# Routing tiles of a gated cross-attention and expert block: the order of q, root, Exp and route transposes

## What is computed

```python
x = x + tanh(g_xattn) * xattn(layernorm(x), ctx)
x = x + tanh(g_ffn) * ffn(layernorm(x))

def xattn(q, ctx):                       # 16 heads of 16, per token
    k, v = split(ctx @ W_kv.T + b_kv)
    attn = softmax(einsum('bshd,bstd->bsht', q, k) / 4)   # heads against heads of the same token
    return einsum('bsht,bstd->bshd', attn, v) @ W_out.T + b_out

def ffn(x):                              # expert choice: 8 experts, each takes 64 of 256 tokens
    probs = softmax(x @ gate_w.T)
    g, m = top_k(probs.T, 64)            # per batch and expert
    h = gelu(x[m] @ w1[e]) @ w2[e]
    return zeros.at[m].add(g * h)
```

## Time and profile before

| what | value |
|---|---|
| median of 3 runs | 736.58 us (736.11 to 738.33) |
| profiled execution | 736.63 us, its span 734.6 us |
| granted TensorE clock, mean | 0.928 of full |
| busy: TensorE matmul | 641.7 us (87%) |
| busy: VectorE | 619.9 us (84%) |
| busy: GpSimd | 550.1 us (75%) |
| busy: ScalarE | 434.1 us (59%) |

### The profile page before, as it was taken

The page is one execution under the profiler, slowest core; times in us unless marked ns, Lnnn a source line. Parts: engine busy times, 40 slices in busy tenths (PEclk is TensorE's granted clock), DMA queues, the critical chain, the costliest instruction groups (busy, mean ns, idle before and its releaser), DMA issues.

```text
span 734.6 us, 10843 instructions
## 1 busy us (share of the span) xinstructions
PE 641.7 (87%) x3592; PEld 514.2 (70%) x3592; DVE 619.9 (84%) x726; ACT 434.1 (59%) x1077; POOL 550.1 (75%) x497
## 2 busy tenths in 40 slices
PE   5668786654799999997999999979999999999994
PEld 2334333322678888775888888758888889999994
DVE  4999999999999999889999999899999461577762
ACT  5477767643577777855777777657776533233320
POOL 3888888888868888698888887888888625445534
PEclk9988898655699999998999999989999999999997
DMA  6967774322367778766887777577777868999972
GB/s 177 345 231 259 263 242 188 125 99 75 123 182 247 237 230 231 224 201 175 243 237 230 230 237 231 185 218 206 235 229 219 268 174 271 317 308 314 308 217 29
DMA packets 97068, 160.90 MB, mean 219 GB/s; under 512 B 8171, under 2 KB 74486, under 8 KB 97014
## 3 DMA queue, kind: packets, MB, share of 16 engines
q1 hardware_dynamic: 84150, 142.91, 58.9%
q0 software_dynamic: 12288, 16.79, 12.1%
q10 hardware_dynamic: 576, 0.52, 0.2%
HBM read 126.63 MB, written 33.55 MB: 218 GB/s over the span
## 4 chain that ended last, share of the span: by engine, by line
PE 55%; DVE 21%; DMA 9%; issue 7%; POOL 6%; ACT 2%; POOLq 0%; ACTq 0%; DVEq 0%
PE bank L1017 20%; PE bank L998 20%; DVE prod_v L459 9%; DMA out_dram<-ys,ids 7%; DVE co L461 5%; PE bank L925 5%; DVE S L461 4%; PE bank L945 3%; POOL prod_p L313 2%; PE bank L986 2%; PE bank L908 2%; DMA xg<-xn_scratch,ids 1%; POOL tree_a L319 1%; POOL out_dram L379 1%; PE bank L957 1%
## 5 line engine op out<-in xcount | busy, mean ns | idle before, releaser
L998 PE MATMUL bank<-xin,w1in 128*128 128x256 f32 x1536 | 206.4, 292 | 7.6 <-issue 4.7
L998 PEld LDWEIGHTS bank<-xin,w1in 128*128 128x128 f32 x1536 | 195.8, 198 | 9.1 <-issue 8.7
L1017 PE MATMUL bank<-w2s,hT 128*128 128x256 f32 x768 | 175.4, 382 | 0.0
L379 POOL DMA_INDIRECT out_dram<-ys,ids x64 | 110.0, 1719 | 76.2 <-ACT ys L748 57.8
L1017 PEld LDWEIGHTS bank<-w2s,hT 128*128 128x128 f32 x768 | 142.4, 190 | 17.8
L738 ACT ACTIVATE hT<-bank 128x512 f32<-128x512 f32 x128 | 76.5, 598 | 117.9 <-PE bank L998 117.5
L461 DVE TENSOR_REDUCE co<-prod_v 128x208 f32<-128x3328 f32 (+2 forms) x32 | 109.7, 3428 | 1.1
L459 DVE TENSOR_TENSOR prod_v<-bank,Ex 128x3328 f32<-128x3328 f32 (+2 forms) x32 | 109.5, 3423 | 0.1
L313 POOL TENSOR_TENSOR prod_p<-kvs,q 128x1024 f32<-128x1024 f32 (+2 forms) x32 | 94.6, 2955 | 14.5 <-ACT q L706 14.5
L459 DVE TENSOR_TENSOR prod_v<-bank,q 128x3072 f32<-128x3072 f32 (+2 forms) x32 | 98.1, 3066 | 6.6 <-ACT q L706 6.6
L461 DVE TENSOR_REDUCE S<-prod_v 128x192 f32<-128x3072 f32 (+2 forms) x32 | 98.2, 3070 | 1.1
(11 more groups left out here) (123 smaller groups left out, 1079.9 us busy)
## 6 DMA issues: line engine op xcount, KB each, us to landing
w1in<-w_parts SPq DMA_DIRECT2D x128, 512.0 KB, 5.6
w2s<-in_L_ffn_w_dram SPq DMA_DIRECT2D x32, 1024.0 KB, 6.1
w_parts<-w1s SPq DMA_DIRECT2D x32, 512.0 KB, 3.5
w1raw<-in_L_ffn_w_dram SPq DMA_DIRECT2D x32, 256.0 KB, 4.4
ct<-in_ctx_dram SPq DMA_DIRECT2D x32, 128.0 KB, 4.5
xt<-in_x_dram SPq DMA_DIRECT2D x32, 128.0 KB, 4.6
out_dram<-x SPq DMA_DIRECT2D x32, 128.0 KB, 4.3
xn_scratch<-xn SPq DMA_DIRECT2D x32, 128.0 KB, 2.8
```

The lines of the kernel that those rows point to most:

```text
L379: pool.indirect_dma_start(out=out_rows[:, :], out_offset=bass.IndirectOffsetOnAxis(ap=ids[:, g % 2, p * E + e:p * E + e + 1], axis=0), in_ ...
L998: ins = pe.matmul(HB[k % 2][:, D * f:D * (f + 1)], w1in[:, k, w, c, P * f:P * (f + 1)].bitcast(f32r), xin[:, n % 2, x_, c, :], start=(m == ...
L1017: ins = pe.matmul(dst, hT[:, n % 2, f, cols], w2s[:, n % 2, f, :], start=(f == 0), stop=(f == FC - 1))
```

## The change

In routing tiles and in the step before one:

- GpSimd: `rsqrt(s + 1)` moves from before the product of `scores(s)` to between its product and its tree.
- ScalarE, step before a routing tile (s = 17, 25): `make_q(s + 1)` moves from behind `take_logits` to ahead of `take_xnT`; `gate_exp` moves ahead of `x2_stats`, with an `exp_warm` added ahead of it. At s = 9 `gate_exp` moves ahead of `take_ctT` and `x2_stats`.
- ScalarE, routing tile: `make_q(s + 1)` and `exp_warm` move ahead of `take_xnT`, `exponentials(s)` ahead of the Gelus 2 and 3, `x2_stats` ahead of `take_y`.
- TensorE, routing tile: `route_columns` moves from behind `logits` to between `hidden(n, 2)` and `hidden(n, 3)`.

```diff
--- before.py
+++ after.py
@@ -305,12 +305,14 @@
 
         @block.gpsimd
         def _(pool):
-            def share(heads, in0, in1, dst, n_tree, done):
+            def share(heads, in0, in1, dst, n_tree, done, root=None):
 
                 full = [P, heads, DK, DK]
                 in0, in1 = in0.unsqueeze(1).broadcast_to(full), in1.unsqueeze(2).broadcast_to(full)
                 pv = prod_p[:, 0:heads * DK * DK].rearrange("p (h a b) -> p h a b", a=DK, b=DK)
                 pool.tensor_tensor(pv, in0, in1, ALU.mult).then_inc(prodp_s, 1)
+                if root is not None:
+                    rsqrt(root)
                 pool.wait_ge(prodp_s, n_tree + 1)
                 src = prod_p[:, 0:heads * DK * DK].rearrange("p (r b) -> p r b", b=DK)
                 for k, buf in enumerate((tree_a, tree_b, tree_c)):
@@ -341,7 +343,7 @@
                 pool.wait_ge(kvs_ready, t + 1)
                 if t > 0:
                     pool.wait_ge(Sc_ready, t)
-                share(H - hk, Kv, qi, S[:, hk * DK:H * DK], 2 * t, Sp_done)
+                share(H - hk, Kv, qi, S[:, hk * DK:H * DK], 2 * t, Sp_done, t + 1 if routing(t) else None)
 
             def values(t):
                 hc = heads(t)[1]
@@ -416,8 +418,6 @@
             rsqrt(0)
             pool.wait_ge(bias_moved, 3 * 16)
             for s in range(NT):
-                if routing(s):
-                    rsqrt(s + 1)
                 scores(s)
                 if not routing(s):
                     rsqrt(s + 1)
@@ -808,11 +808,11 @@
                     take_low(s, 3)
                 if s >= 2:
                     take_logits(s - 2)
+                if routing(s + 1):
+                    gate_exp(s // TG - 1)
                 take_ctT(s + 2)
                 if s >= 1:
                     x2_stats(s - 1)
-                if routing(s + 1):
-                    gate_exp(s // TG - 1)
             for s in range(N0 - 1, NT):
                 n = s - N0
                 if routing(s):
@@ -824,17 +824,17 @@
                     take_kv(s + 1)
                     make_xn(s - 2)
                     x_stats(s + 2)
+                    make_q(s + 1)
+                    act.activation(exp_warm[:, :], tanh_g[:, 0:1], ACT.Exp)
                     take_xnT(s - 2)
+                    exponentials(s)
                     if n >= 0:
                         gelu(n, 2)
                         gelu(n, 3)
                     take_logits(s - 2)
-                    make_q(s + 1)
-                    act.activation(exp_warm[:, :], tanh_g[:, 0:1], ACT.Exp)
-                    exponentials(s)
+                    x2_stats(s - 1)
                     if n >= 1:
                         take_y(n - 1)
-                    x2_stats(s - 1)
                     take_xh(n + 1)
                     continue
                 if s + 1 < NT:
@@ -850,15 +850,18 @@
                 make_xn(s - 2)
                 if s + 2 < NT:
                     x_stats(s + 2)
+                if routing(s + 1):
+                    make_q(s + 1)
                 take_xnT(s - 2)
                 gelu(n, 2)
                 gelu(n, 3)
                 take_logits(s - 2)
-                if s + 1 < NT:
+                if routing(s + 1):
+                    act.activation(exp_warm[:, :], tanh_g[:, 0:1], ACT.Exp)
+                    gate_exp(s // TG - 1)
+                elif s + 1 < NT:
                     make_q(s + 1)
                 x2_stats(s - 1)
-                if routing(s + 1):
-                    gate_exp(s // TG - 1)
                 if n >= 1:
                     take_y(n - 1)
             n = n1 - 1
@@ -1088,10 +1091,11 @@
                 xn_transposes(s - 2)
                 if n >= 0:
                     hidden(n, 2)
+                if routing(s):
+                    route_columns(s // TG - 1)
+                if n >= 0:
                     hidden(n, 3)
                 logits(s - 2)
-                if routing(s):
-                    route_columns(s // TG - 1)
                 if n >= 1:
                     outputs(n - 1, 1)
                 if routing(s):
```

## The result

| | changed kernel | kernel before | ratio, 95% interval |
|---|---|---|---|
| first measurement | 729.99 us (727.61 to 730.63, 4 runs) | 737.46 us | 0.9888 (0.9849 to 0.9926) |
| second, `after_again` below | 726.75 us (726.27 to 727.19, 4 runs) | 736.74 us | 0.9864 (0.9846 to 0.9882) |

The change is 7.5 us faster in one measurement and 10.0 in the other, against 7.1 forecast. The profiled execution of the first took 727.61 us (span 725.6), 9.0 less than the one of the kernel before; it was the fastest of its four. Its timelines run 0.9 us later from the first tiles on (`con` of tile 17 ends at 309.4 and not at 308.5), so 0.9 must be taken off its times where they are set beside those of before.

The account below looks back on a forecast made before the run. TensorE bounds ordinary stretches; around routing tiles 18 and 26 VectorE's chain does, with GpSimd's ending close ahead. Removing two waits, 2 x (2.20 + 1.36) = 7.1 us, from 736.6 gave 729.5; range 725.5 to 733.0.

Parts of the forecast that it names:

- The two waits: Tiles 18 and 26: VectorE's waits for ScalarE's Exps ahead of `gsum` (2.20 us) and `den` (1.36) go, 7.1 us in all.
- One bound: Tile 18: tokens copied about 331.9, low part due 331.94; if GpSimd's chain ended last, the gain is 3.03, not 3.56.
- Both chains must shorten: Routing tiles: GpSimd's gather chain ends only some 2 us ahead of VectorE's, so a gain needs both shorter.
- a remark: Tile 18: the gather, issued earlier, no longer starts under the two additions or beside the w2 load; 3.56 us taken.
- The rival by which a change of table costs as much again: ScalarE: the gate's Exp gains 1.0 us instead of 2.2 in two tiles, giving 732.0; chance 0.04.
- TensorE's clock: Rival: behind the gaps of tiles 18 and 26 the clock stays at 2.4 GHz, 2.3 and 1.4 us more, 725.8; chance 0.17.
- a fall one stage early: Rival: the route transposes' wait, if over about 1.5 us, halves TensorE's clock from hidden 3 on, giving 740.7; chance 0.05.
- Tile 10: Tile 10: GpSimd already waits for `ids` and VectorE has no wait to lose; 0 gained, bounds -0.3 and +0.3 us.

Follow-up runs that it names:

- after_again: The changed kernel once more, unedited: 726.75 us, 10.0 us under the kernel before.
- undo_gate_exp: Changed kernel with the gate's Exp back behind the statistics, without the tiny Exp: 730.63 us, 3.9 us slower than the changed kernel.
- undo_exp_ahead: Changed kernel with the scores' Exp and the tiny Exp back behind Gelus 2 and 3 and the logits' copy: 736.25 us.
- only_q_root: Kernel before with only q ahead of the transposed copy and the root between product and tree: 735.47 us, -1.4 to before.
- only_gate_exp: Kernel before with only the gate's Exp and the tiny Exp ahead of the statistics: 740.70 us, +3.8 to before.
- undo_root: Changed kernel with the root back ahead of the 12-head product: 744.31 us, +7.6 to the kernel before.
- undo_root_w2_late: Changed kernel with the root back ahead of the product and, in routing tiles, the w2 load held until the gather has landed: 737.08 us.
- before_fill: Kernel before with 24 and 10 extra matmuls, results unread, around the token transposes of tiles 18 and 26: 733.23 us, -3.7 to before.
- undo_route: Changed kernel with TensorE's route transposes back behind logits: 730.85 us, 3.9 us slower than the changed kernel.
- heads2_gather_first: Changed kernel; in routing tiles VectorE takes 2 heads' scores, GpSimd 14, and the output additions come behind the weighted values: 735.25 us.
- heads3: Changed kernel; in routing tiles VectorE takes 3 heads' scores and GpSimd 13: 729.34 us, 2.1 us slower than the changed kernel.

## Why the prediction was right, and where it was not

**The two waits.** Right, as forecast. With 0.9 us taken off for the later start, the changed kernel's trace has the 12-head product at 304.1 (304.2 forecast), the gather at 324.5 (324.55), `hidden` at 332.6 (332.7), and 0.76 us of wait at the route transposes (0.6). `undo_gate_exp` and `undo_exp_ahead` bring back waits of 1.38 and 2.87 us. One bound was less close than forecast: I had the tokens copied just when VectorE's low part is due, with the 4.93 us of the earlier trace rows. The transfer took 3.96, and the copy ended about 1 us ahead of the low part (331.70 and 332.75).

**Both chains must shorten.** Right, and stronger than I had it. GpSimd's part alone gains 1.4 us (`only_q_root`), the gate's Exp alone loses 3.8 (`only_gate_exp`), and all of the change but the root's new place loses 7.6 (`undo_root`). The size of a late gather was wrong in what I expected of `undo_root`: I priced it by its delay, and the trace showed that it also meets the w2 load and takes 7.1 us. What I had given as a remark, that the gather no longer runs beside that load, is worth 4 us a tile once the gather is that late (`undo_root_w2_late`).

**The tables.** The rival by which a change of table costs as much again is out. In the changed kernel's rows above, the load of 1.28 at 324.87 begins 0.02 us after the Exp ends, and the Gelu starts at 326.17, 0.02 us after the load; the trace does not bear out the drain of about 1.38 us given by the Trainium skill (ScalarE: Activation LUTs, "What ACT_TABLE_LOAD costs"). The measured row decides.

**TensorE's clock.** This is the step that failed. I gave 0.17 to the case that the clock stays at 2.4 GHz in both tiles, took it as falling in the sum, and argued from one row: a fall after an idle time of 1.50 us. Both profiled executions of the changed kernel show 3.10 to 3.12 us in both tiles, and `before_fill` prices it at 3.7, as the rival did (2.3 + 1.4). The argument from the earlier trace rows does not hold even for its own place. In `undo_route`, TensorE waits the same 1.50 us in tile 11 and the clock stays at 1.00 (197 to 201 us). Its timeline:

```profile
196.57 0.44 PE L911 MATMUL bank<-ident,xn 128*128 128x128 f32 x2 [1.50 <-ACT xn L715]
196.76 3.12 PE L1001 MATMUL bank<-xin,w1in 128*128 128x256 f32 x24
```

So one row with a fall was no ground for a fall elsewhere. The other way by which the clock could cost, a fall one stage early once the wait at the route transposes is near 1.5 us, did not come in the changed kernel (0.76), and came in tile 26 of `undo_gate_exp` (1.50), though not in its tile 18 (1.51) and without the loss that I had priced. What exactly decides was not tried.

**The ledger.** In the profiled executions: 0.9 late start lost, 3.6 + 3.6 from the two chains, 2.3 + 1.4 from the clock, and some 1.0 given back behind the two tiles, where TensorE waits for `xn` (0.5 in each, shown above). That makes 9.0, as the spans do. The part given back was not in my sum. That it goes back to GpSimd's late values by way of `con` and `Sc` is read from the rows; no run tests it.

**The point.** The forecast of 729.5 lies half a microsecond from the first median and 2.8 from the second, whose value fits the clock case (725.8) less the part given back. That the first median came so close is luck: the sum had left out the 3.7 of the clock and the 1.0 given back, and three of that measurement's four runs took 2 to 3 us more than the profiled one. Why they did stays open, since there are no rows for them. The 1.2 us of tile 12 and the 1.1 of the last stretch, which differ between the traces, are of that size together, but nothing shows that it was they.

**Tile 10.** Right: its gather waits for `ids` as before, and nothing is gained; TensorE's transposes of `xn` came 0.2 us later there.

## What to carry to other kernels

Where two engines' chains end close together, work both out, and expect a change of one alone to gain nothing or to lose: here the root and q for GpSimd alone gave -1.4 us, the change without the root's new place +7.6, and the whole -10.0. A gap in front of dense matmuls can have a second price, the half clock in the matmuls behind it, here 2.3 and 1.4 us beside the 3.6 of each tile's waits; it is measured by filling the gap with matmuls whose result nobody reads. And before shifting more work to the engine with slack, look at what its next DMA will run beside. When a trace is used to explain a difference in the total, compare it tile by tile: here 3.5 us of `undo_root`'s loss arose in tiles that its expectation did not look at.

## What the runs showed that I had not expected

The length of TensorE's last wait does not decide alone whether its clock falls. In `undo_gate_exp` the token transposes end and `hidden` starts 2.24 us of idle time later in tile 18, as in the changed kernel (2.25), and yet the group took 4.60 us there against 3.10:

```profile
324.21 0.63 PE L974 MATMUL bank<-ident,lists 32*128 32x32 f32 x4 [1.51 <-DVE lists L557]
...
334.09 4.60 PE L1000 MATMUL bank<-xin,w1in 128*128 128x256 f32 x24 [2.24 <-issue]
```

The first row shows what differs: 10 us earlier TensorE had waited 1.51 us, against 0.76 in the changed kernel. It is not the only candidate, for in `heads2_gather_first` the clock fell behind a gap of 3.5 us, shorter than the changed kernel's 3.7, with no wait at the route transposes at all (hidden 4.59). And TensorE's same wait of 1.50 us in tile 11 ended with either clock.

An indirect gather of the same 128 rows took from 2.9 to 7.1 us from issue to TensorE's start: 2.9 with the w2 load held, 4.0 in the changed kernel, where the w2 load is issued 3.2 us behind it, 5.0 in the kernel before, where it is issued 0.7 us behind, 6.0 in `heads3`, and 7.1 in `undo_root`, where it is issued 0.35 us ahead. Only the step from 7.1 to 2.9 is from an edit that moves nothing but that load.
